# Unread identity products on TensorE during the layer norms of a nine-stage vision tower

## The reference

```python
h = _L0_tok_ref(x, L0_tok_W)                       # patches, FFT, embedding
h = concatenate([cls_tok, h])
h = h + _L0_attn_ref(_layernorm(h), ...)           # RWKV recurrence
h = h + _L0_ffn_ref(_layernorm(h), ...)            # mixture of depths
h = h + _L1_attn_ref(_layernorm(h), ...)           # linear attention
h = h + _L1_ffn_ref(_layernorm(h), ...)            # grouped attention, top-2 experts
h = h + _L2_attn_ref(_layernorm(h), ...)           # causal attention, head size 2
h = h + _L2_ffn_ref(_layernorm(h), ...)            # switch experts
h = h + _L3_attn_ref(_layernorm(h), ...)           # attention by distance
h = h + _L3_ffn_ref(_layernorm(h), ...)            # experts with capacity
```

## Time and profile before

| | us |
|---|---|
| median of 3 runs | 1702.46 |
| the runs | 5573.35, 1698.28, 1702.46 |
| the profiled execution | 1708.56 |
| its span, first instruction to last | 1706.7 |

### The profile page before, as it was taken

One profiled execution on the slowest core, in us unless ns is written; L12 is line 12 of the kernel. 1 busy time (PEld: TensorE's weight loads), 2 busy tenths in 40 slices (PEclk: granted clock), 3 DMA queues, 4 the chain that ended last, 5 costly groups with the idle time before them and its releaser, 6 DMA issues. The chain is left out here.

```text
span 1706.7 us, 28456 instructions
## 1 busy us (share of the span) xinstructions
PE 1324.1 (78%) x11389; PEld 750.3 (44%) x11389; DVE 1025.4 (60%) x1996; ACT 861.2 (50%) x1752; POOL 366.7 (21%) x405
## 2 busy tenths in 40 slices
PE   8648993940357965995699999867899999985995
PEld 2437993730344433554233333344455444564442
DVE  2467556821699137666566464444599999965233
ACT  0321221220220743334899999721599999972121
POOL 0000410000031220000000000000299999950000
PEclk9776997565665886996699999968699999996898
DMA  9000000013200000000000000001000000001000
GB/s 116 8 6 15 1 2 8 1 40 37 47 2 1 1 15 1 1 1 2 2 2 1 2 2 2 1 10 23 8 2 2 2 2 2 2 2 28 1 1 12
DMA packets 71211, 17.58 MB, mean 10 GB/s; under 512 B 65248, under 2 KB 70511, under 8 KB 71073
## 3 DMA queue, kind: packets, MB, share of 16 engines
q1 hardware_dynamic: 71080, 15.78, 5.8%
HBM read 13.67 MB, written 2.10 MB: 9 GB/s over the span
## 5 line engine op out<-in xcount | busy, mean ns | idle before, releaser
L2811 POOL TENSOR_SCALAR da_AD<-di_QH,di_KH 128x256 f32<-128x256 f32 x320 | 287.5, 919 | 52.7 <-POOLq L2590 47.4
L2796 ACT ACTIVATE da_AD<-ps,di_NK 128x256 f32<-128x256 f32 x760 | 288.2, 841 | 0.4
L2772 DVE TENSOR_TENSOR da_AD<-ps,di_KH 128x1024 f32<-128x1024 f32 x240 | 273.2, 1220 | 0.8
L2156 ACT ACTIVATE pt_PT<-ps 128x1024 f32<-128x1024 f32 x288 | 266.3, 1103 | 8.3 <-PE ps L2226 7.9
L2847 PE MATMUL ps<-da_AD,da_win 128*32 128x256 f32 x4080 | 241.6, 384 | 19.6 <-ACT da_AD L2796 15.0
L2847 PEld LDWEIGHTS ps<-da_AD,da_win 128*32 128x32 f32 x4080 | 123.0, 110 | 133.7 <-ACT da_AD L2796 40.4
L2192 PE MATMUL ps<-pt_PT,pa_V 128*32 128x512 f32 (+3 forms) x1536 | 158.0, 506 | 8.5 <-DVE pt_Yc L2133 3.2
L2140 DVE TENSOR_TENSOR pt_PT<-pt_PT,pt_keep 128x512 f32<-128x512 f32 x128 | 84.3, 690 | 62.8 <-ACT pt_PT L2156 61.7
L2226 PE MATMUL ps<-pt_QT,pt_KT 12*128 12x512 bf16 (+3 forms) x768 | 80.1, 337 | 2.8 <-DVE pt_KT L2098 0.5
L2524 PE MATMUL ps<-cp_XT,cp_W 96*128 96x342 f32 x192 | 72.5, 504 | 0.0
L2350 POOL MEMSET sw_xo<- 114x576 f32 x1 | 0.6, 578 | 334.3 <-POOLq L147 334.3
(11 more groups left out here) (701 smaller groups left out, 2372.5 us busy)
## 6 DMA issues: line engine op xcount, KB each, us to landing
em_xs<-in_x_dram SPq DMA_DIRECT2D x4, 1024.0 KB, 10.4
la_scratch<-la_qkv SPq DMA_DIRECT2D x3, 513.0 KB
la_blk<-la_scratch SPq DMA_DIRECT2D x24, 64.1 KB
ew_win<-in_L_ffn_w_dram SPq DMA_DIRECT2D x4, 320.0 KB
cp_W<-in_L_ffn_w_dram SPq DMA_DIRECT2D x2, 512.0 KB
dp_tokrow<-in_c_tokenrow_dram SPq DMA_DIRECT2D x1, 513.0 KB
mt_exf<-in_c_expand_dram SPq DMA_DIRECT2D x1, 510.0 KB
out_dram<-h SPq DMA_DIRECT2D x2, 228.0 KB
```

The source lines that it names most:

```text
L2156: nc.scalar.activation(PT[:, n % RING, 2 * i:2 * i + 2, :], ps[:, b0:b0 + 2, :], ACT.Exp, scale=SCALE).then_inc(exp_ok, 1)
L2772: nc.vector.tensor_tensor(AD[:, n % RING], bc(QD[:, u % 2], 4), bcl(kk, SELP), ALU.max).then_inc(ad_dve, 1)
L2796: ins = nc.scalar.activation(AD[:, n % RING, q], QA[:, u % 2], ACT.Abs, bias=NK[:, u, s:s + 1])
L2811: ins = nc.gpsimd.tensor_scalar(AD[:, n % RING, q], QH[:, u], KH[:, u, s:s + 1], None, ALU.max)
```

## The change

A new function issues `n` products of the identity with itself into columns 0 to 127 of PSUM bank 5. It waits for nothing and signals nothing, and nobody reads the result: every later use of bank 5 begins with an instruction that overwrites it.

```diff
+def keep_clock(nc, K, n, bank=5):
+
+    for _ in range(n):
+        nc.tensor.matmul(K.ps[:, bank, 0:128], K.ident[:], K.ident[:], start=True, stop=True)
```

It is called once in PE's program of eight functions, right before PE waits for the norm (`routed` runs twice, so nine times in an execution, 246 products):

```diff
 rwkv_projections
+                keep_clock(nc, K, 24)
                 pe.wait_ge(x_ready, 1)
 rwkv_output
+                keep_clock(nc, K, 38)
                 pe.wait_ge(o_ok, 1)
 stage_depths
+                keep_clock(nc, K, 24)
                 pe.wait_ge(x_ok, 1)
 stage_linear, behind pe.wait_ge(c_in, 128) and the three transposes L1081
                 ins.then_inc(wt_ps, 1)
+                keep_clock(nc, K, 24)
                 pe.wait_ge(x_ok, 1)
 gqa_attention, behind pe.wait_ge(c_in, 160) and L1322, L1323
+                keep_clock(nc, K, 40)
                 pe.wait_ge(x_ok, 1)
 the pair stage's preparation, behind pe.wait_ge(c_in, 64) and L1996, L1997
+                keep_clock(nc, K, 24)
                 pe.wait_ge(x_ok, 1)
 routed
+                keep_clock(nc, K, 24)
                 pe.wait_ge(x_ok, 1)
 distance_prepare, behind pe.wait_ge(c_in, 208) and L2685, L2686
+                keep_clock(nc, K, 24)
                 pe.wait_ge(sel_ok, NT)
                 pe.wait_ge(x_ok, 1)
```

## The result

The changed kernel takes 1710.47 us (median; 1704.54 to 1737.31), the kernel before 1701.61 us beside it. The ratio is 1.0058 with a 95% interval from 1.0038 to 1.0078: about 9.9 us, 0.6%, slower. The ratio counts only executions within 1.5% of the fastest of their kernel, so 1737.31 and before's 5573.35 are not in it. The forecast was 1704, a little slower. The profiled execution took 1709.53 us with a span of 1707.7, only 1.0 us more than before's 1706.7: the profiled execution of before (1708.56) is one of that kernel's longer ones.

The account below looks back on a forecast made before the run. TensorE, busy 78% with a clock swinging between 1.2 and 2.4 GHz, can gain from clock where a stage waits for it. Terms sum to +1.9 us on a median of 1702.46: 1704 us, own range 1694 to 1714, with rivals 1691 to 1718.

Parts of the forecast that it names:

- Price of a product: Everywhere: each product leaves two records, of 0.213 us each at the low clock and 0.107 at the high one.
- Nothing gained in projections and output: Products there fit inside the norm wait with idle time behind them: 0 each, bounds -2.5 and -1.5 us.
- Depth stage, -1.5: Products hidden in the 8.6 us wait; clock falls after them or work behind runs fast: -1.5 us (0 to -7).
- Linear stage, +0.8: Products 4.7 us late, 0.9 back from transposes, and 5.4 back in the 5 of 9 cases without a lucky clock rise.
- Attention, +2.5: Grouped attention: 40 products end 4.4 us late, 1.9 back from faster transposes and records, net +2.5 us.
- Pair stage, -0.6: Products end 3.9 us late, but work behind them runs at the high clock: -0.6 us (+3.9 to -2).
- Distance, +4.5: Distance stage: products stand before work ready after 1 us, so its matmuls end later: +4.5 us (3.7 to 5.1).
- Routed stages, -3.8: Switch and capacity stages: products hidden in the wait, gate matmuls and transposes faster, -1.9 us each (0 to -4.3).
- A: Rival, everywhere: the high clock survives the idle remainder of the waits; -17.4 us, 1685 us, chance 0.15.
- B: Rival: the clock is gone when the real work comes, only delays are left; +17.5 us, 1720 us, chance 0.12.
- C: Rival: the products don't raise the clock and take their low-clock time; +40.6 us, 1743 us, chance 0.03.
- D: Rival: nothing happens, products idle away in cover; 1702 us, chance counted within the forecast's 0.68.

Follow-up runs that it names:

- e2_gated: The changed kernel with only the products behind DMA-gated weight transposes kept (linear, attention, pair, distance); 1712.75 us, ratio 1.0069 to the kernel before.
- e1_covered: The changed kernel with products kept only where PE waits for the norm alone (projections, output, depth, routed); 1699.35 us, ratio 1.0004 to the kernel before.
- e10_routed: The kernel before with only the 24 products ahead of the norm in the routed blocks; 1693.46 us, ratio 0.9952.
- e11_linear_pair: The kernel before with only the products of the linear and the pair stage; 1703.51 us, ratio 1.0029.
- e8_attention: The kernel before with only the 40 products of the grouped attention; 1705.26 us, ratio 1.0011.
- e7_distance: The kernel before with only the 24 products of the distance stage; 1708.62 us, ratio 1.0032.
- e4_transposes: The changed kernel with its products replaced by transposes, twice as many; 1721.39 us, ratio 1.0129 to the kernel before.
- e5: e3_moved with a second burst in projections, output and depth, released by the norm's variance signal; 1690.98 us, ratio 0.9919 to the kernel before.
- e9: e5 plus products in the pauses before and among the routed experts, and four more bursts in attention and pair stage; 1673.05 us, ratio 0.9823 to before.
- e3_moved: The changed kernel with the products of the four gated blocks issued before the DMA wait; 1700.95 us, ratio 0.9984 to the kernel before.

## Why the prediction was right, point by point

The direction was right, and 1710.5 lies in the range of 1691 to 1718. The sum was too kind: +1.9 us was forecast and +9.9 came. By halves, the gated terms add up to +7.2 (0.8 + 2.5 - 0.6 + 4.5) and e2_gated cost 11.7; the covered terms add up to -5.3 (-1.5 - 1.9 - 1.9) and e1_covered cost 0.7. So the larger part of the miss is in the covered half: a gain in the routed stages that e10_routed has and that doesn't appear beside the other covered products. The prediction priced the gate matmuls there and left out the experts behind them, whose clock moves those blocks by more than any term of the sum (capacity 157 to 171 us in the 14 profiles, switch 57 to 88). That the time still fell in the range owes something to the range's width of 27 us.

The terms measured alone don't add up to the whole either: 5.5 + 1.9 + 4.9 - 8.2 is +4.1 us, and the rest up to 9.9 stays without a place. "With" and "without" below are block lengths averaged over the profiles whose kernel does or doesn't have that place's product where the change puts it.

- *Price of a product.* 48 records in 5.60 us at 1.00 are 0.117 us, not 0.107. The weight loads, 128 columns wide, fill 5.38 of it; L834's were 114, which is the likely reason and was not tested. A tenth more on every fast product.
- *Nothing gained in projections and output.* Right: the low stretches of the earlier trace rows are low again, and the block lengths agree to 1 us.
- *Depth stage, -1.5.* The mechanism was right, and the branch that the prediction named first came each time: products at the high clock, then a gap in which it falls. The block was 60.58 to 60.59 us in every profile without a bridge, so the term is 0 and the gain booked for the other branch was not there.
- *Linear stage, +0.8.* Of the gated terms this one was furthest off. The delay was right (transposes at 364.95, norm ready near 360.8: 4.1 us for the 4.7 forecast). What I paid back for "luck" was not there. With products the block is 93.25 to 96.33 us (five profiles, mean 94.5), without 90.47 to 92.33 (six, mean 91.1): +3.4. In all six profiles without these products, L1091 took 6.11 us, the fast value. A 4 in 9 read over different places of one trace was taken for a chance at each place; here it came every time, in the depth stage never. The blocks make that 2.8 us for e11_linear_pair (+3.4 here, -0.6 in the pair stage) where 0.2 was forecast; it cost 2.4 us by the medians and 4.9 by the ratio, to which three of its twelve executions, at 1715 to 1718 us, add.
- *Attention, +2.5.* The 80 records took 11.7 us for 10.8 forecast and the transposes came 5 us after the norm. Blocks: 335.1 with, 332.4 without; e8_attention +1.9. Right.
- *Pair stage, -0.6.* 3.9 us late, as forecast; L2021 then took 5.46 us for 32 records, 10.61 before. Blocks 332.4 with, 333.0 without (before's own 336.6 left out as the odd one; with it 333.6). Right to about 1 us.
- *Distance, +4.5.* L2705 ran at 1.00 (36 records in 7.94 us) and ended 26.9 us into the block; before, as L2691, it ended 22.2 us in, so it is 4.7 us late. e7_distance cost 5.5 us. Blocks 366.9 with, 361.2 without, though the five with spread from 361.5 to 374.4: in e2_gated and e4_transposes the same matmuls ended 3 us late and the block is as long as without products. Right in kind, 1 us short.
- *Routed stages, -3.8.* Gate matmuls 3.8 us for 36 records, 7.15 before; with 22 of 36 fast, as forecast, it would have been 4.9. e10_routed gained 8.2; inside the changed kernel the gain can't be told from what the experts' clock does.
- *Rivals.* A (the clock carries) was wrong for this change and right about the prize: e5 and e9 earned it with other placements. B's pure delay of 17.5 us is more than e2_gated's 11.7, and its premise failed: in the four gated places the clock was high when the real work came. C, products that don't raise the clock, is out: they raised it in each place where it was low. D, nothing happens, is out by the interval.

## What to carry to other kernels

Work that only holds a clock must be out of the way when the real work comes and must reach close to it. Put it behind no wait that can be late (here the DMAs), and tie its last burst to a signal shortly before the one waited for, not to a count. The first took the loss of 10 us away (e3_moved), the second made a gain of it (e5_bridged). Look for the places where a pause ends in long dense work: 33 products before and among the experts gave more than 246 before the norms. And a low-clock stretch is worth filling only where PE sets the end: in e5_bridged's depth block the last 23 us ran at 0.50, and DVE was the one that was full. Where a block's time hangs on the clock, compare several profiles and block by block; one pair can mislead.

## What the runs showed of the hardware

- f32 transposes alone raise the clock, and at the same speed as matmuls: 48 in 7.95 us at a mean of 0.68, 48 product records in 7.99 us at the same mean in the same block.
- With the clock low, expert matmuls that keep PE busy 59.38 of 60 us left it low to the end (e4_transposes), while the same code ran at 1.00 in most other profiles. In the switch block, once it was high, they held it to the end in every profile where it rose. So a stage of 60 us can hang on the state in which it begins.
- The clock outlived PE's last work by some 3 us in the projections and by 2.4 us in the depth stage, 0.5 us before the next work; in e4_transposes it was lost within 0.2 us of PE's last work before the switch block (1.00 up to 1111.70, 0.54 over 1111.70:1113.50). How long a pause it survives is not a constant in these traces.
